# A fused layer in eight blocks: the router chooses from its logits, the early tiles' output accumulations wait by slot, and the queues are reordered from step 8

## The reference

```
h = layernorm(x) * (1 + cb) + sb
scores = softmax(h @ router_w)                       # (4096, 8)
expert_weights, expert_idx = top_k(scores, 2)
h_e = gelu(h @ w1[e]) * (h @ v1[e]);  y_e = h_e @ w2[e]     # F = 704
out = sum over the two chosen e of expert_weights * y_e + bias
x = x + gb * out
```

## Time and profile before

| what | value |
|---|---|
| runs | 873.79, 866.54, 871.64 us, median 871.64 |
| profiled execution | 868.28 us, its span 866.5 us |
| TensorE's mean granted clock | 0.978 of full speed |
| PE / DVE / POOL / ACT busy | 820.7 / 566.7 / 490.9 / 373.8 us |
| longest wait of PE behind 297 us | 5.76 us, at 402.99 to 408.75 us |

### The profile page before, as it was taken

The page is one execution under the profiler, slowest core; times in us unless marked ns, Lnnn a source line. Parts: engine busy times, 40 slices in busy tenths (PEclk is TensorE's granted clock), DMA queues, the critical chain, the costliest instruction groups (busy, mean ns, idle before and its releaser), DMA issues.

```text
span 866.5 us, 19016 instructions
## 1 busy us (share of the span) xinstructions
PE 820.7 (95%) x5027; PEld 729.7 (84%) x5028; DVE 566.7 (65%) x1569; ACT 373.8 (43%) x679; POOL 490.9 (57%) x458
## 2 busy tenths in 40 slices
PE   6889999999999899797999999999999999999994
PEld 4678898989889788586989999999999999999993
DVE  6678777878876858885555655656555555656552
ACT  4775656565664514342423324234234343342230
POOL 2363745868685865675844745647437465374333
PEclk9999999999999999798999999999999999999997
DMA  8031050303021261156242422423424312222221
GB/s 280 26 112 49 1 177 1 124 25 100 13 88 44 82 195 52 45 198 177 68 116 42 141 48 37 136 41 89 99 37 134 49 37 43 37 37 48 38 37 18
DMA packets 49421, 67.61 MB, mean 78 GB/s; under 512 B 4896, under 2 KB 43680, under 8 KB 49376
## 3 DMA queue, kind: packets, MB, share of 16 engines
q1 hardware_dynamic: 35712, 47.71, 17.7%
q0 software_dynamic: 13664, 19.35, 11.4%
HBM read 43.51 MB, written 23.54 MB: 77 GB/s over the span
## 4 chain that ended last, share of the span: by engine, by line
PE 81%; POOL 7%; DMA 4%; issue 3%; DVE 3%; ACT 1%; DVEq 0%; POOLq 0%; SPq 0%; ACTq 0%
PE ps L593 23%; PE ps L594 23%; PE ps L595 23%; PE ps L754 5%; POOL routed L1882 3%; DMA out_rows<-y_moe,tok_moe 3%; PE ps L720 2%; POOL split L403 1%; PE ps L693 1%; PE ps L775 1%; PE ps L774 1%; PE ps L639 1%; PE ps L611 1%; POOL y_moe L1893 1%; PE ps L681 1%
## 5 line engine op out<-in xcount | busy, mean ns | idle before, releaser
L593 PE MATMUL ps<-split,xT_moe_hi 128*128 (+2 forms) x426 | 167.9, 394 | 0.6 <-DVE split L403 0.6
L594 PE MATMUL ps<-split,xT_moe_lo 128*128 (+2 forms) x426 | 161.7, 380 | 0.0
L595 PE MATMUL ps<-split,xT_moe_hi 128*128 (+2 forms) x426 | 161.4, 379 | 0.0
L1893 POOL TENSOR_TENSOR y_moe<-y_moe 128x256 f32<-128x256 f32 x71 | 72.3, 1018 | 120.9 <-DVE y_moe L1561 120.9
L1104 ACT ACTIVATE hidT_hi<-ps 128x768 fp32r<-128x768 f32 x71 | 57.6, 812 | 163.3 <-PE ps L754 163.3
L1899 POOL DMA_INDIRECT out_rows<-y_moe,tok_moe x71 | 111.1, 1565 | 28.6 <-issue 28.2
L593 PE MATMUL ps<-split,hidT_hi 128*128 (+1 forms) x355 | 106.6, 300 | 3.5 <-issue 2.3
L1098 ACT ACTIVATE gelu_moe<-ps 128x704 f32<-128x704 f32 x71 | 53.8, 758 | 124.0 <-PE ps L595 122.0
L594 PE MATMUL ps<-split,hidT_lo 128*128 (+1 forms) x355 | 100.7, 284 | 0.0
L595 PE MATMUL ps<-split,hidT_hi 128*128 (+1 forms) x355 | 100.7, 284 | 0.0
L1561 DVE SCALAR_TENSOR_TENSOR y_moe<-ps,gate_moe,gates 128x256 f32<-128x256 f32 x142 | 62.1, 479 | 57.6 <-PE ps L775 54.1
(11 more groups left out here) (219 smaller groups left out, 1956.1 us busy)
## 6 DMA issues: line engine op xcount, KB each, us to landing
raw<-in_w SPq DMA_DIRECT2D x9, 1408.0 KB
x_moe<-routed SPq DMA_DIRECT2D x74, 132.5 KB
raw<-in_w SPq DMA_DIRECT2D x9, 640.0 KB
x_sb<-in_x SPq DMA_DIRECT2D x8, 512.0 KB, 3.7
x_again<-in_x SPq DMA_DIRECT2D x8, 512.0 KB, 4.4
out_rows<-x_again SPq DMA_DIRECT2D x8, 512.0 KB, 3.0
gu_raw<-in_gu_t SPq DMA_DIRECT2D x1, 1536.0 KB, 7.3
raw<-in_w SPq DMA_DIRECT2D x18, 64.0 KB
```

Of the source, the lines that this page charges most:

```text
L593: pe.matmul(dst, a_hi, b_hi, start=first, stop=False)
L594: pe.matmul(dst, a_lo, b_hi, start=False, stop=False)
L595: return pe.matmul(dst, a_hi, b_lo, start=False, stop=last)
L1893: g.tensor_tensor(y_moe[:, t.slot, 0, :], y_moe[:, t.slot, 0, :], y_moe[:, t.slot, 1, :], ALU.add)\
```

## The change

Three things are changed.

**The router's order.** `choose(q)` takes the 8 sorted values and the indices from the logits in PSUM, subtracts the largest for the exponential, and writes the masks' sum straight as bfloat16. `count(q)` adds the block to the running counts, which are now kept in two copies. `weigh(q)` sums the exponential, divides and writes the weights into the rows. `slots(q)` keeps only the row numbers. The ranking waits for the choice and the counts, not for the exponential; the scatter waits for row numbers and weights. In `step(r)` of DVE, `hidden(r-1, 0)` comes first, then the whole of `choose` ahead of the first scan, and nothing of the router between the two scans.

**The accumulations.** The semaphore `added` becomes one per slot. `take_gates` and `gate_y` wait for their own slot. `add_rows` of tiles 1 to 4 waits for no other accumulation; tile 5 waits for all of them, and each later tile for the one before, as it was.

**The queues from step 8.** All four engines' lists are written in a new order, with one bank order (`RING_TAIL`) that follows. The number of instructions of the large kinds is the same; SP's list is unchanged. The three functions that go (`softmax_start`, `top2`, `place_top2`) stand above.

```diff
-        gate_steps, gates_r, y_sum, added = sem("gate_steps"), sem("gates_r"), sem("y_sum"), sem("added")
+        gate_steps, gates_r, y_sum = sem("gate_steps"), sem("gates_r"), sem("y_sum")
+        added = [sem(f"added{n}") for n in range(SLOTS)]
...
-                pe.wait_ge(slots_r, q + 1)
+                if q >= 1:
+                    pe.wait_ge(slots_r, q)
...
             def rank_tokens(q):
 
                 pe.wait_ge(chosen_r, q + 1)
+                pe.wait_ge(seen_r, q + 1)
...
-                pe.wait_ge(slots_r, NBLK + 1)
-                pe.matmul(total, ones[:], seen_b[:], start=True, stop=True).then_inc(total_mm, 1)
+                pe.wait_ge(slots_r, NBLK)
+                pe.wait_ge(seen_r, NBLK + 1)
+                pe.matmul(total, ones[:], seen_b[:, NBLK % 2, :], start=True, stop=True).then_inc(total_mm, 1)
...
             gate_up(7, 11)
             router_logits(5)
+            first_products(Tile(0), PICKED, AB[:2])
+            rank_tokens(5)
+            ffn_out(7, 0)
+            ffn_out(7, 1)
             h2_transposes(6, 0)
-            x_transposes(Tile(0))
-            ffn_out(7, 0)
-            rank_tokens(5)
+            first_products(Tile(0), PICKED, AB[2:])
             h2_transposes(6, 1)
-            ffn_out(7, 1)
+            x_transposes(Tile(1))
             router_logits(6)
-            first_products(Tile(0), PICKED, AB[:2])
-            first_products(Tile(0), PICKED, AB[2:])
-            rank_tokens(6)
-            x_transposes(Tile(1))
             hid_transposes(Tile(0))
             first_products(Tile(1), PICKED, AB[:2])
-            h2_transposes(7, 0)
+            first_products(Tile(1), PICKED, AB[2:])
             x_transposes(Tile(2))
-            h2_transposes(7, 1)
-            router_logits(7)
-            first_products(Tile(1), PICKED, AB[2:])
             second_product(Tile(0), PICKED)
+            rank_tokens(6)
             hid_transposes(Tile(1))
             first_products(Tile(2), PICKED, AB[:2])
+            h2_transposes(7, 0)
+            h2_transposes(7, 1)
+            first_products(Tile(2), PICKED, AB[2:])
+            router_logits(7)
+            x_transposes(Tile(3))
+            second_product(Tile(1), PICKED)
             rank_tokens(7)
-            x_transposes(Tile(3))
-            first_products(Tile(2), PICKED, AB[2:])
             count_all()
-            second_product(Tile(1), PICKED)
             hid_transposes(Tile(2))
             first_products(Tile(3), PICKED, AB[:2])
             first_products(Tile(3), PICKED, AB[2:])
+            second_product(Tile(2), PICKED)
             x_transposes(Tile(4))
-            second_product(Tile(2), PICKED)
             table_transposes()
             hid_transposes(Tile(3))
             first_products(Tile(4), PICKED, AB[:2])
             first_products(Tile(4), PICKED, AB[2:])
+            second_product(Tile(3), PICKED)
             x_transposes(Tile(5))
-            second_product(Tile(3), PICKED)
 
...
-            ROUTE = 11
-
...
+            ROUTE = 4
+
+            def choose(q):
 
                 v.wait_ge(logit_mm, q + 1)
                 link = chain(route, q * ROUTE)
                 for i in range(TPB):
+                    a = v.max(top[:, i, :], logits[:, i, :])
                 link(a)
                 for i in range(TPB):
+                    a = v.max_index(top_i[:, i, :], top[:, i, :], logits[:, i, :])
                 link(a)
+                v.tensor_tensor(zz[:], logits, top[:, :, 0:1].to_broadcast([P, TPB, E]), ALU.subtract).then_inc(z_r, 1)
                 link(v.tensor_copy(top_f[:], top_i[:, :, 0:2]))
                 iota = cn[:, C_IOTA:C_IOTA + TPB * E].rearrange("p (i e) -> p i e", e=E)
                 for k in range(2):
+                    a = v.tensor_tensor(hot[:, k], iota, top_f[:, :, k:k + 1].to_broadcast([P, TPB, E]), ALU.is_equal)
+                link(a)
+                v.tensor_tensor(chosen_b[:], hot[:, 0], hot[:, 1], ALU.add).then_inc(chosen_r, 1)
+
+            def count(q):
+
+                v.wait_ge(chosen_r, q + 1)
+                link = chain(seen_steps, q * 2)
+                link(v.tensor_reduce(seen_add[:], chosen_b[:].rearrange("p i e -> p e i"), AX.X, ALU.add))
+                link(v.tensor_tensor(seen[:], seen[:], seen_add[:], ALU.add))
+                v.tensor_copy(seen_b[:, (q + 1) % 2, :], seen[:]).then_inc(seen_r, 1)
+
+            def weigh(q):
+
+                v.wait_ge(exp_r, q + 1)
+                if q >= 2:
+                    v.wait_ge(scattered[q % 2], q // 2 * 32 * TPB + 16)
+                link = chain(weigh_steps, q * 3)
+                link(v.tensor_reduce(mx[:], ee[:], AX.X, ALU.add))
+                v.tensor_copy(rows[:, q % 2, :, D + E], tok_f[:, q % 2, :])
+                link(v.reciprocal(mx[:], mx[:]))
+                v.wait_ge(chosen_r, q + 1)
+                link(v.tensor_tensor(pp[:], ee[:], mx[:].unsqueeze(2).to_broadcast([P, TPB, E]), ALU.mult))
+                v.tensor_scalar(tok_f[:, q % 2, :], tok_f[:, q % 2, :], float(BLK), None, ALU.add)
+                v.tensor_tensor(rows[:, q % 2, :, D:D + E], chosen_b[:], pp[:], ALU.mult).then_inc(weighed, 1)
+
+            SLOT = 3
...
-                v.tensor_copy(slot_i[:, q % 2], slot_f[:])
-                link(v.tensor_reduce(seen_add[:], chosen[:].rearrange("p i e -> p e i"), AX.X, ALU.add))
-                link(v.tensor_tensor(seen[:], seen[:], seen_add[:], ALU.add))
-                v.tensor_copy(seen_b[:], seen[:]).then_inc(slots_r, 1)
+                v.tensor_copy(slot_i[:, q % 2], slot_f[:]).then_inc(slots_r, 1)
...
-                    v.wait_ge(added, (t.v - SLOTS + 1) * 16)
+                    v.wait_ge(added[t.slot], t.round * 16)
...
+                if on(r - 1):
+                    hidden(r - 1, 0)
                 if on(r - 3):
-                    softmax_start(r - 3)
-                if on(r - 1):
-                    hidden(r - 1, 0)
+                    choose(r - 3)
                 if on(r):
                     scan(r, 0)
-                if on(r - 3):
-                    top2(r - 3)
                 if on(r):
                     scan(r, 1)
                 if on(r - 2):
                     add_ffn(r - 2, 0)
                 if on(r - 3):
-                    place_top2(r - 3)
+                    count(r - 3)
+                    weigh(r - 3)
                 if on(r - 2):
...
             norm2_centre(6)
+            split_lo(v, PICKED, 0)
+            hidden(7, 4)
+            xT_rest(Tile(0))
+            split_lo(v, PICKED, 1)
+            hidden(7, 5)
+            choose(5)
+            split_lo(v, PICKED, 2)
+            slots(5)
+            take_gates(Tile(0))
+            weigh(5)
+            add_ffn(7, 0)
+            take_gates(Tile(1))
             norm2_scale(6)
-            hidden(7, 4)
-            hidden(7, 5)
-            softmax_start(5)
-            take_gates(Tile(0))
-            top2(5)
-            place_top2(5)
-            xT_rest(Tile(0))
-            slots(5)
-            take_gates(Tile(1))
-            split_lo(v, PICKED, 0)
-            take_gates(Tile(2))
-            add_ffn(7, 0)
-            split_lo(v, PICKED, 1)
-            softmax_start(6)
             add_ffn(7, 1)
+            count(5)
+            multiply(Tile(0))
             gate_xo(7)
-            top2(6)
-            take_gates(Tile(3))
-            multiply(Tile(0))
-            place_top2(6)
+            xT_rest(Tile(1))
+            choose(6)
+            hidT_rest(Tile(0))
             norm2_stats(7)
-            xT_rest(Tile(1))
+            multiply(Tile(1))
+            xT_rest(Tile(2))
             norm2_centre(7)
             norm2_scale(7)
-            hidT_rest(Tile(0))
             slots(6)
-            xT_rest(Tile(2))
-            split_lo(v, PICKED, 2)
-            softmax_start(7)
-            multiply(Tile(1))
-            top2(7)
-            place_top2(7)
+            weigh(6)
+            gate_y(Tile(0))
+            count(6)
             hidT_rest(Tile(1))
+            choose(7)
+            xT_rest(Tile(3))
+            count(7)
+            take_gates(Tile(2))
             slots(7)
-            gate_y(Tile(0))
             multiply(Tile(2))
-            xT_rest(Tile(3))
+            weigh(7)
+            gate_y(Tile(1))
+            split_lo(v, 0, 2)
+            hidT_rest(Tile(2))
             table()
-            hidT_rest(Tile(2))
-            gate_y(Tile(1))
+            xT_rest(Tile(4))
             multiply(Tile(3))
             split_lo(v, 0, 0)
-            xT_rest(Tile(4))
             table_out()
+            hidT_rest(Tile(3))
             gate_y(Tile(2))
             split_lo(v, 0, 1)
-            hidT_rest(Tile(3))
             multiply(Tile(4))
             xT_rest(Tile(5))
-            split_lo(v, 0, 2)
+            take_gates(Tile(3))
+            gate_y(Tile(3))
             take_gates(Tile(4))
-            gate_y(Tile(3))
             hidT_rest(Tile(4))
```

(18 more changed lines are left out.)

93 lines of the change are left out of this document (38 added, 55 removed).

## The result

The changed kernel takes 861.97 us (median of 9 runs, 859.83 to 864.32), the kernel before 870.10 (9 runs, 865.58 to 873.79): a ratio of 0.9911, 95% interval 0.9887 to 0.9935, 8.1 us less. The forecast was 857 on 871.64, 14.6 less, of which the sum gave 13.3 and the remaining 1.3 has no source; the range, 847 to 867, holds the time. The profiled execution took 862.0 us, its span is 860.2 where it was 866.5. (A ratio is taken from runs that stand beside each other in time, so it is not exactly the quotient of the two medians; 0.9911 of 870.1 would be 7.7 us less. One run of the kernel before, at 1364.56 us in a later session, counts in no ratio.)

A forecast was written before the change was run, and what follows sets the result against it. Only PE's stalls and low clock between 297 and 441 us could be saved, at most about 30 us. Terms -1.4 - 4.4 - 4.9 + 4.7 - 7.3 = -13.3 us gave 858.3 from 871.64, stated as 857; range 847 to 867.

The forecast's parts named there:

- The rival of the choice ahead of the first scan: Steps 3 to 7: choose delays the carry, PE stands at the state transposes; +10 us, some 880; chance 0.08.
- main case: The whole change: the forecast itself, 11 to 17 us less; chance 0.45.
- step 4: Last count and table: PE waits for the ranking, slots and take_gates, then the table; costs +4.7 us, bounds 0 and +9.
- Step 1: Second norm, wait for xn2T_lo: POOL's base addition moves away, DVE's four products end sooner; -1.4 us, bounds 0 and -2.9.
- Step 2: Wait for hid_lo at block 7's gate and up groups goes, with low clock behind; -4.4 us, bounds -5.4 and -2.
- Step 3: Ranking of block 6: its wait goes as the choice needs only the logits; -4.9 us, bounds -8.4 and 0.
- Step 5: Accumulations of tiles 1 to 4 without the serial chain: tile 5's hid_moe wait goes; -7.3 us, bounds -8 and 0.
- the landing beside the weights: Rival "the landings stay": the 9.0 us landing comes from weight transfers, step 5 gives nothing; -6 us, some 864; chance 0.13.
- The rival "DVE becomes the bound": About 355 to 388 us: DVE can't keep up, half of steps 2 and 3 returns in step 4; some 861; chance 0.15.
- faster by over 1%: Whole kernel under 862.9 us; chance 0.75, summed from the forecast, the case above it and parts of two rivals.

The follow-up runs named there:

- r2: The changed kernel run again, unaltered, in a later session: 855.01 us against 867.11 for the kernel before, ratio 0.9870.
- r1: The changed kernel run again, unaltered, in a later session: 853.94 us against 867.01 for the kernel before, ratio 0.9864.
- e1: The kernel before with the accumulations' semaphore by slot and nothing else: 866.75 us, ratio 1.0002 to the kernel before.
- e2: The changed kernel with each accumulation of tiles 1 to 4 waiting again for the one before: 862.23 us, ratio 0.9948 to the kernel before.
- e9: The kernel before with the accumulations' semaphore by slot and block 7's base moved behind tile 1's add_rows: 859.73 us, ratio 0.9920 to the kernel before.
- e3: The changed kernel's router and accumulations, with all engines' queues behind step 7 in the old order: 866.30 us, ratio 0.9999 to the kernel before.
- e10: The changed kernel with block 7's base put back ahead of tile 0's accumulation: 856.47 us, ratio 0.9889 to the kernel before.
- e8: The changed kernel with the last and early counts later on PE, multiply of tiles 2 and 3 earlier on DVE: 863.61 us, ratio 0.9936 to before.

## Why the prediction was right, and where it was not

**The place and the sign** were right: steps 3 to 7 and the loop did not move, all came from the 144 us between. The rival of the choice ahead of the first scan was rightly small: in step 7 the carry copies start at 283.74 (284.02 before), since what went ahead of the first scan left the space between the two.

```profile
283.74 0.20 DVE L1421 COPY carry<-sg_sb 128x1 f32<-128x1 f32 x2
```

**The size.** 13.3 us were forecast by the sum, 8.1 measured; 13.1 and 12.1 in the later sessions. So the range held, but the first measurement lies outside the main case (11 to 17 less), which the two later ones meet. The term that was mis-sized in the first is step 4: +4.7 forecast, +10.3 measured, with +5.7 in r2. Its idle terms were a little small in both (2.1 against 3.3 and 2.5 at the count; 1.3 against 3.2 and 1.5 at tile 3). The rest is clock: one low window of 1.7 was allowed, 6.5 were lost, 4.0 of them behind the norm that came 1.0 us late when a scatter landed late. Nothing in the sum allowed for a late landing at any place but that of tile 5. That r1 and r2 come near the 13.3 is in part luck: their profiled executions lack the low clock at 33 to 37 us, 1.4 us that no step of the prediction is about.

**Step 1** gave 1.1 of its 1.4 at `xn2T_lo` and lost that again just behind. Its low clock was left out of the sum: in the kernel before the clock was at the lower level from 302.7 to 306.1 us too, 1.7 us behind this wait (the mean of 300 to 307 us is 0.76), and that went. The mechanism was right, the four products take 2.35 us instead of 4.28; but POOL's addition to the base did not go away, it now meets the row numbers of block 4, which `count_early` waits for:

```profile
296.77 2.35 DVE L1471 SCALAR_TENSOR_TENSOR rows<-rows,rstd,mod 128x256 f32<-128x256 f32 x4
...
301.05 3.06 DVE L1525 TENSOR_TENSOR pos_k<-pos,hot 128x32 f32<-128x32 f32 x2
```

```profile
301.69 2.37 POOL L1871 TENSOR_TENSOR x_again<-x_again,mod 128x1024 f32<-128x1024 f32 x1
```

Two small products that take 0.29 us elsewhere (and 1.98 at this place before) take 3.06, and PE waits 1.5 us at `count_early` (L793). "Ask what the moved operation meets next" was not asked. **Step 2** came out as said for `hid_lo`. The clock's loss in the first piece went from 3.4 to 0.0, half of it step 1's and half step 2's.

**Step 3** was forecast at -4.9. With the rest of step 2 its piece was to give -7.2, and gave -6.8, and -8.1 in r2.

**Step 5** has the right size, -7.6, and half a reason; that the size came out is luck to that extent. I said that everything hung on the serial chain, and gave the landing beside the weights 0.13 as a rival. e1 shows that rival in full: without the chain and with the old order nothing is won. It takes both, no chain (e2: 8 us lost with it, nearer to 6 by the waits) and an issue well ahead of the weights (e9: 7.4 us won by that, once the chain is gone). "The change moves the base behind tile 1" stood in the text as a detail; it was half of the term.

**The rival "DVE becomes the bound"** predicted 8.6 less by half of steps 2 and 3 returning in step 4. The first measurement, 8.1 less, is nearer to it than to the forecast, and the growth of step 4 looks like it; but in r2 step 4 is near its forecast, and in the first the growth is clock and waits of which a part (2.3 us at the ranking) fell while DVE stood idle. What e3 shows is its mechanism in small: a wait taken from PE at one place of DVE's queue is found again at the next.

**The chances.** 0.75 stood on faster by over 1%, and the first measurement is 0.9%, the two later ones 1.4% and 1.3%. The two further table loads on ACT were free as far as PE's longer waits show: none of those listed ends at a function behind one.

**The sums.** Redone, some don't come out. The five single waits make 15.1 us, not 16 (16 is nearer to their rows' totals). In step 3, 1.3, 0.4 and 1.7 are 3.4, not 3.5. The forecast, 857, and all of the rivals' times lie about 1.3 us under 871.64 less their own sums, for no reason given. DVE as the bound is 871.64 - 8.6 = 863.0, which is not under 862.9, so most of its 0.13 did not belong to "faster by over 1%"; and a fifth of the landings' 0.13 is 0.03, not 0.05.

## What to carry over

Where a queue issues small transfers whose landing is awaited, look at what else is on its way at that time, not only at what the issue waits for: an accumulation landed in 3.9 us when it was issued 2.9 us ahead of the weights (e10) and in 9.0 to 10.7 beside them, and taking away its wait alone was worth nothing. In a stretch where PE waits for one in-order queue at several places, price an exchange by the next item in that queue that is awaited; the accumulations alone and with the router gave 0, and with one call of POOL moved the accumulations gave 7.4. Before a difference between two executions is put down to a place, lay the same instructions side by side from the start: windows at fixed times compare different work once one execution is ahead. And measure a change of about 1% in more than one session.

## What was not expected of the hardware

- The same program was 8.1, 13.1 and 12.1 us faster than its predecessor in three sessions, with intervals of some 2 us to each side; the kernel before moved by 3 us between sessions, the changed one by 8.
- A clock at the lower level for 8 us (0.50 from 365 to 373) in which PE was busy all the time, behind a stretch of 4 us in which it was busy 2.2. And one of 3.4 us at 33 us, in the kernel's first block, that some executions of one program have and others don't.
- Up to 5.1 us between the record of a ranking's last matmul and its consumer, with DVE and ACT idle (e8), and nothing in the profile to say why.
- POOL's addition to the base (2.4 us) held up three kinds of DVE instructions that met it, and not only products of two operands: 2.35 became 4.28, 0.29 became 3.06, and in r2, where the row numbers came 1.4 us sooner, it was the cast behind them that paid:

```profile
300.80 1.98 DVE L1530 CAST slot_i<-slot_f 128x8 int32<-128x8 f32 x1
```

A cast of 8 columns that takes 0.17 elsewhere takes 1.98. The Trainium skill, page "SBUF — State Buffer", section "SBUF: two separate sides", names both kinds, operations with two SBUF inputs and those in a two-port mode; this case's rows agree.
